# Order of the two norms, the router and the LoRA turn in eight steps of a fused two-block attention kernel, and another instruction for the softmax bias

## The reference

```python
x = x + jnp.tanh(g_xattn[0]) * _L0_xattn_ref(_layernorm(x), ctx_4096, ...)  # 32 heads, 8 kv heads of 128, rms-normed q and k
x = x + jnp.tanh(g_ffn[0]) * _L0_ffn_ref(_layernorm(x), A, B, Wr, br)       # 8 experts of rank 16, softmax router
x = x + jnp.tanh(g_xattn[1]) * _L1_xattn_ref(_layernorm(x), ctx_4096, ...)  # 16 heads, 4 kv heads of 96
x = x + jnp.tanh(g_ffn[1]) * _L1_ffn_ref(_layernorm(x), W_gate, W_up, W_down)  # silu(gate) * up, 1792 wide
```

## Time and profile before

| | us |
|---|---|
| median of 3 runs | 1187.22 (1186.21 to 1187.59) |
| the profiled execution's own time | 1187.59 |
| its span, first to last instruction | 1185.8 |
| PE busy | 1126.9 (95%) |
| DVE busy | 854.2 (72%) |
| ACT busy | 825.2 (70%) |
| POOL busy | 371.1 (31%) |
| mean granted TensorE clock | 0.989 of full speed |

### The profile page before, as it was taken

The page is one execution under the profiler, slowest core; times in us unless marked ns, Lnnn a source line. Parts: engine busy times, 40 slices in busy tenths (PEclk is TensorE's granted clock), DMA queues, the critical chain, the costliest instruction groups (busy, mean ns, idle before and its releaser), DMA issues.

```text
span 1185.8 us, 22717 instructions
## 1 busy us (share of the span) xinstructions
PE 1126.9 (95%) x7184; PEld 710.5 (60%) x7184; DVE 854.2 (72%) x2066; ACT 825.2 (70%) x2695; POOL 371.1 (31%) x669
## 2 busy tenths in 40 slices
PE   6689999999999999999999998799999999799998
PEld 4445666666666666666666655566766766455554
DVE  5577767767767667777677789998888888743434
ACT  5678888888888888878888766677787765522221
POOL 5454434334733333333343454322111121000000
PEclk8899999999999999999999999999999999999999
DMA  7366654463655545555445746668996786200000
GB/s 246 101 126 138 130 125 101 119 143 85 139 147 120 116 109 126 129 104 131 119 99 116 143 98 134 136 140 171 232 189 144 136 173 122 49 1 1 36 1 36
DMA packets 411992, 139.56 MB, mean 118 GB/s; under 512 B 386656, under 2 KB 396640, under 8 KB 411872
## 3 DMA queue, kind: packets, MB, share of 16 engines
q1 hardware_dynamic: 409968, 134.43, 51.7%
q0 software_dynamic: 1904, 3.67, 1.1%
HBM read 39.21 MB, written 2.10 MB: 35 GB/s over the span
## 4 chain that ended last, share of the span: by engine, by line
PE 80%; DVE 10%; ACT 3%; issue 3%; POOL 2%; DMA 1%; DVEq 0%; POOLq 0%; ACTq 0%
PE bank L518 23%; PE bank L519 22%; PE bank L520 22%; PE bank L719 8%; PE bank L738 4%; DVE pieces L1079 1%; DVE mx L1182 1%; ACT probs L901 1%; DVE stats L1090 1%; DVE x L1219 1%; ACT junk L810 1%; DVE lg L1237 1%; DVE xn L1102 1%; POOL rstd L1474 1%; DVE q_rows L1079 1%
## 5 line engine op out<-in xcount | busy, mean ns | idle before, releaser
L807 ACT ACTIVATE pieces<-probs,rs 128x256 f16<-128x256 f32 x384 | 166.0, 523 | 10.4 <-DVE rs L1199 9.0
L1182 DVE TENSOR_REDUCE mx<-bank 128x2 f32<-128x512 f32 x192 | 131.5, 685 | 55.6 <-PE bank L520 55.4
L901 ACT ACTIVATE probs<-bank,nb,rq 128x256 f32<-128x256 f32 x256 | 141.1, 563 | 41.1 <-DVE nb L1187 40.6
L1079 DVE SCALAR_TENSOR_TENSOR pieces<-probs,rs,pieces 128x256 f16<-128x256 f32 x384 | 163.2, 485 | 5.6 <-ACT pieces L807 4.8
L518 PE MATMUL bank<-wq,xT 128*128 128x512 f16 (+1 forms) x384 | 139.5, 363 | 2.7 <-DVE wq L1079 2.7
L810 ACT ACTIVATE junk<-bank 128x128 bf16<-128x128 f32 x384 | 101.6, 287 | 55.2 <-PE bank L520 55.2
L518 PE MATMUL bank<-wo_hi,oT 128*128 128x512 f16 x352 | 134.0, 381 | 5.7 <-DVE oT L1079 4.3
L519 PE MATMUL bank<-wq,xT 128*128 128x512 f16 (+1 forms) x384 | 139.4, 363 | 0.0
L520 PE MATMUL bank<-wq,xT 128*128 128x512 f16 (+1 forms) x384 | 139.2, 363 | 0.0
L519 PE MATMUL bank<-wo_lo,oT 128*128 128x512 f16 x352 | 134.2, 381 | 0.0
L520 PE MATMUL bank<-wo_hi,oT 128*128 128x512 f16 x352 | 134.1, 381 | 0.0
(11 more groups left out here) (185 smaller groups left out, 2638.7 us busy)
## 6 DMA issues: line engine op xcount, KB each, us to landing
raw_o<-in_wo_a SPq DMA_DIRECT2D x8, 1024.0 KB, 6.0
raw_q<-in_wq_a SPq DMA_DIRECT2D x7, 1024.0 KB, 6.0
raw_kv<-in_wkv_a SPq DMA_DIRECT2D x8, 512.0 KB, 3.8
turned<-pieces SPq DMA_TRANSPOSE x192, 2.8
raw_q<-in_wq_c SPq DMA_DIRECT2D x4, 768.0 KB, 5.1
raw_o<-in_wo_c SPq DMA_DIRECT2D x4, 768.0 KB, 4.9
down_rest<-in_down_t POOLq DMA_DIRECT2D x5, 512.0 KB, 4.2
ff_in<-in_gate_t SPq DMA_DIRECT2D x4, 448.0 KB, 4.2
```

Source lines behind the costliest of these rows:

```text
L807: return act.activation(out, in_, ACT.Copy, scale=scale)
L901: act.activation(probs[:, h, :], bank[h // 2][:, (h % 2) * KV:(h % 2 + 1) * KV], ACT.Exp, bias=nb[:, h:h + 1], scale=scale, accum_out=sums ...
L1079: return dve.scalar_tensor_tensor(out, in_, scale, hi, ALU.mult, ALU.subtract)
L1182: dve.tensor_reduce(mx[:, pr], chunks(bank[i][:, :], 2), AX.X, ALU.max, negate=True).then_inc(mx_done, 1)
```

## The change

The stages of `step(n)` are put in another order on each engine, and the bias nb is made by other instructions. On DVE `norm_scale(2)` goes ahead of the router, `row_max(S, 1)` ahead of `lora_scale`, `lora_low` ahead of `probs_low(S, 0)`. On POOL and SP the stages of norm2 go ahead of those of norm1. On ACT `norm_row_hi(2)` goes ahead of `norm_row_hi(1)` and `router_exp`, and `lora_act_hi` ahead of `probs_high(S, 0)`. On PE `lora_turn` goes ahead of `project(Y)`. The tile `zeros` and its memset go away.

```diff
 @block.sync step:
+                if norm2 is not None:
+                    turn_norm(2, norm2)
                 if norm1 is not None:
                     turn_norm(1, norm1)
-                if norm2 is not None:
-                    turn_norm(2, norm2)
 @block.tensor step:
+                if lora is not None:
+                    lora_turn(lora)
                 if Y is not None:
                     project(Y)
-                if lora is not None:
-                    lora_turn(lora)
                 values(n)
 @block.scalar step:
+                if norm2 is not None:
+                    norm_row_hi(2, norm2)
                 if norm1 is not None:
                     norm_row_hi(1, norm1)
                 if lora is not None:
                     router_exp(lora)
-                if norm2 is not None:
-                    norm_row_hi(2, norm2)
...
+                if lora is not None:
+                    lora_act_hi(lora)
                 if norm3 is not None:
                     norm_hi(3, norm3)
                 if S < N:
                     probs_high(S, 0)
-                if lora is not None:
-                    lora_act_hi(lora)
-                if S < N:
                     probs_high(S, 1)
 @block.vector row_max:
-                    dve.scalar_tensor_tensor(nb[:, pr], mx[:, pr], 1.0, rq[:, c:c + 2], ALU.mult, ALU.mult
-                                             ).then_inc(nb_done, 1)
+                    dve.tensor_tensor(nb[:, pr], mx[:, pr], rq[:, c:c + 2], ALU.mult).then_inc(nb_done, 1)
...
-                    dve.scalar_tensor_tensor(nb[:, pr], mx[:, pr], es[:, g % 2, s:s + 1], zeros[:, :], ALU.mult, ALU.add
-                                             ).then_inc(nb_done, 1)
+                    dve.tensor_scalar(nb[:, pr], mx[:, pr], es[:, g % 2, s:s + 1], None, ALU.mult).then_inc(nb_done, 1)
 @block.vector step:
                 if norm1 is not None:
                     norm_scale(1, norm1)
-                if lora is not None:
-                    norms_of_step(n)
-                    router_logits(lora)
                 if norm2 is not None:
                     norm_scale(2, norm2)
                 if norm3 is not None:
                     norm_scale(3, norm3)
+                if lora is not None:
+                    norms_of_step(n)
+                    router_logits(lora)
                 if S < N:
                     row_max(S, 0)
                 if lora is None:
                     norms_of_step(n)
+                if S < N:
+                    row_max(S, 1)
                 if lora is not None:
                     lora_scale(lora)
-                if S < N:
-                    row_max(S, 1)
...
+                if lora is not None:
+                    lora_low(lora)
                 if norm3 is not None:
                     norm_low(3, norm3)
                 if S < N:
                     probs_low(S, 0)
-                if lora is not None:
-                    lora_low(lora)
-                if S < N:
                     probs_low(S, 1)
 @block.gpsimd step:
+                if norm2 is not None:
+                    norm_rstd(2, norm2)
                 if norm1 is not None:
                     norm_rstd(1, norm1)
-                if norm2 is not None:
-                    norm_rstd(2, norm2)
                 if norm3 is not None:
                     norm_rstd(3, norm3)
                 if norm0 is not None:
                     norm_rows(0, norm0)
+                if norm2 is not None:
+                    norm_rows(2, norm2)
                 if norm1 is not None:
                     norm_rows(1, norm1)
-                if norm2 is not None:
-                    norm_rows(2, norm2)
 @block.gpsimd, start:
-            pool.memset(zeros[:, :], 0.0).then_inc(consts, 1)
...
-            pool.wait_ge(consts, 9)
+            pool.wait_ge(consts, 8)
```

More of the change, by code:

```diff
@@ L206, in build @@
         half_neg = sb("half_neg", NT)
-        zeros = sb("zeros", 2)
         half_pos = sb("half_pos", NT)
```

## The result

| | before | changed |
|---|---|---|
| median | 1187.46 us (6 runs) | 1194.80 us (6 runs, 1191.94 to 1197.27) |
| ratio, 95% interval | | 1.0061 (1.0048 to 1.0075) |
| profiled execution, span | 1185.8 us | 1193.9 us |
| DVE from the start of step 59's oT to step 67's | 105.3 us | 112.6 us |

The changed kernel is slower by 0.6%, and the time is 0.4 us from the forecast. The parts of the sum are less exact than that: two errors of about 2 us each cancelled, so that the total came so near is luck.

A forecast was written before the change was run, and what follows sets the result against it. DVE was taken to pace steps 59 to 66, PE the rest. Terms +5.9 (steps 61 to 65), +0.75, -0.3, +0.1 and +1.5 (clock) gave +8.0 us, a median of 1195.2 us; range 1190 to 1201.

The forecast's parts named there:

- DVE paces eight steps, PE all others: Steps 59 to 66: a microsecond on DVE moves the end by one; outside them it moves nothing.
- POOL's rstd order: Step start: norm1's rstd queues behind norm2's on POOL, DVE's first xn starts late; loss 1.56 us a step.
- The stretched nb: DVE's two nb fall inside POOL's subtractions: 1.04 instead of 0.57 us and 0.46 instead of 0.16; losses 0.47 and 0.30.
- lg, -0.78: DVE's lg now comes behind both POOL subtractions and runs free of them: gain 0.78 us a step.
- The sum of a step: DVE in steps 61 to 65: v_lo 1.55 us late, less sums_in's wait of 0.37: +1.18 a step, +5.9 in five.
- Step 60: First-layer step: q_low waits for ACT's squares, which end at 9.0 instead of 8.2: +0.75 us.
- The clock: PE's pause before the turn may put project at half clock, y_done late: 0.3 a step, +1.5 us, bounds 0 and 9.
- nb's new instructions: New forms of nb on DVE, 16 of them in steps 59 to 66: taken as 0, at most 3 us either way.
- A: Rival: POOL's subtractions miss nb and lg, step cost +0.2, sum near +1, 1188 us; chance 0.11 (up to 1190).
- C: Rival: PE's waits for tT_lo held the loop and the earlier turn frees it, 1182 us; chance 0.04.
- B: Rival: clock falls in nearly every step, five steps at 1.8 us, 1203 us; chance 0.12 (above 1199).
- -0.37: DVE's wait at sums_in goes, as row_max(S, 1) ahead of lora_scale brings the exponentials earlier: gain 0.37 us a step.

The follow-up runs named there:

- b_nb: Kernel before with only nb's new instructions, zeros kept: 1188.29 us, ratio 1.0000.
- b_rstd: Kernel before with norm2's rstd ahead of norm1's on POOL, nothing else: 1195.01 us, ratio 1.0054.
- a_rstd: Changed kernel with norm1's rstd put back ahead of norm2's on POOL: 1186.57 us, ratio 0.9989.
- a_split: Changed kernel with norm1's rstd first again and nb in steps 59 to 66 made one element per instruction: 1179.90 us, ratio 0.9936.
- a_fill: Changed kernel with 16 filler transposes on PE ahead of the turn in steps 60 to 66, output unread: 1190.67 us, ratio 1.0023.
- a_turn: Changed kernel with lora_turn put back behind project(Y) on PE: 1191.87 us, ratio 1.0029.

## Why the prediction was right

**DVE paces eight steps, PE all others.** Right in the main. Each run that changed DVE's time in steps 59 to 66 by more than 3 us changed its median the same way, by as much to within 3 us; b_nb changed 192 instructions, nearly all elsewhere, and the end stayed. That the stretch behind would be as long as before was not so: it took 1.5 us more.

**POOL's rstd order, +1.56 us a step.** Right in place and cause, shown from both sides by b_rstd and a_rstd. The size was 1.39: the powers were priced at the 0.71 us of the earlier trace rows, where the xn of norm1 ran on DVE beside them. In the changed kernel that xn waits for them, and they take 0.56.

**The stretched nb, +0.47 and +0.30.** Measured 1.04 and 0.48 us against 0.57 and 0.16, so +0.47 and +0.32. **lg, -0.78:** 0.23 instead of 1.01, -0.78. a_split and the changed kernel show that it is the operands that decide whether POOL's subtraction holds an instruction. With two SBUF tensors nb waits (1.04 in step 62). In steps 63 to 65 nb has one SBUF tensor and a scalar in the changed kernel too: with two elements it is held as long (1.04, 0.98, 1.04), with one element in a_split it never is (0.21). lg, of the same kind with eight elements, is held (0.75 in a_split). The first part agrees with the rule of the Trainium skill that the prediction quotes (SBUF — State Buffer, "Who interferes with whom"), which names a second SBUF input and the two-port modes. Counts other than one, two and eight were not run.

**The sum of a step, +1.18.** Mis-sized: steps 62 and 65, with no wait for PE, were 0.72 and 0.67 us longer than before. Beside the 0.17 of the powers, the part between v_lo and y_add was 0.66 us shorter than before, and only 0.37 of that was in the sum: with the exponentials early, DVE's following instructions find ACT's results ready and follow each other without the small gaps. That was 0.5 us a step too much, 2.3 us in five steps. Step 60 measured +0.66 (forecast +0.75), step 59 -0.35 (-0.3), step 66 -0.39 on DVE.

**The clock, +1.5.** Mis-sized the other way. The mechanism was right: a pause of PE in front of the turn, the granted clock at half behind it, y_add late. It fell in three of the five steps and cost 1.2, 0.9 and 1.2 us at y_add and 0.3 at lora_add: 3.5. These three steps are 3.9 us longer than at the +0.7 of the other two, so 0.4 lies in no wait that the profile shows. a_fill and a_turn gave 4.1 and 2.9 back. The price rested on the wait of 2.04 us in step 60 of the kernel before, which the earlier trace rows calls the longest; the longest was 2.61, at 768.20, and no fall stood behind it. PE also left step 66 about 0.6 us later beside DVE, where 0.3 had been said. The two errors, -2.3 and +2.0, cancelled by luck, and so the total was nearer than its parts.

**nb's new instructions, 0.** Right (b_nb, 1.0000).

**The rivals.** A, the reordering pays its own way: its condition wasn't met, since both nb were held in all of the steps 60 to 65. Its price stays untested, since no run has a late rstd and a free nb. a_rstd, early rstd and held nb, is 1.3 us faster than before. C, that the LoRA chain was the pace: refuted, since in the changed kernel PE waits for tT_lo no more and the time went up. B, the clock in every step: it fell in three of five, at up to 1.4 us each (1.2 at y_add, 0.3 at lora_add) and not 1.8.

What the prediction weighed too little is inside its own numbers: -0.78, -0.37 and +0.30 belong to one swap and don't need the others. Taken apart from the norms they were the best edit in the diff.

## What to carry to other kernels

When a reordering bundles several swaps, price each swap alone before the sum: here one of them was worth -0.7%, another +0.5%, and a third cost 3 to 4.5 us where the clock fell as well. On an engine that runs in order, a call that waits for the last work of the step before must not stand ahead of one whose input is long there. And a tiny instruction can be the dear one: look at the spread of its durations, not at the mean, and at who runs beside the slow ones.

## What the hardware showed that was not expected

Pauses of nearly the same length had a fall of the clock behind them or not: 3.37, 3.44 and 2.43 us had (at 712.61, 742.44 and 757.43), 2.81, 2.80 and 2.48 us had none (at 696.90, 727.90 and 772.40). The kernel before had a fall behind a pause of 2.04 us (at 701.25) and none behind one of 2.61 (at 768.20). So the length of the pause alone doesn't tell, and the number of falls may differ between executions of one program. Over the thirteen executions of the changed kernel the slower ones tend to have the lower mean clock (0.989 at 1191.8 us, 0.984 at 1197.3), but the order is loose, and the falls were counted only in the profiled ones. And POOL's power on one element per partition takes 0.56 us with DVE idle beside it, and as much beside DVE's oT, but 0.63 to 0.84 wherever an xn runs beside it (0.71 at 720.02 in the earlier trace rows) and 0.95 beside wo_lo. That DVE's operands hold it, as POOL's hold nb, fits this but was tested by no run.
